# Cross-attention and an FP4 feed-forward layer: FFN rows handled last, the logits' scale moved, FFN weights quantised in five passes, loops written out

## The reference

```python
q = einsum('bnd,hdk->bhnk', layernorm(x), proj_q) + bias_q
k, v = the same of ctx with proj_k, bias_k and proj_v, bias_v
attn = softmax(einsum('bhqk,bhnk->bhqn', q, k) / sqrt(64))
x = x + (attn @ v, heads side by side) @ w_out.T
gate = fp4_linear(layernorm(x), w_gate); up = fp4_linear(layernorm(x), w_up)
x = x + fp4_linear(silu(gate) * up, w_down)
```

## Time and profile before

| | us |
|---|---|
| median of 3 runs | 460.31 (457.93 to 460.86) |
| the profiled execution | 461.22 |
| its span in the profile | 459.4 |
| granted TensorE clock, mean | 0.97 of full |
| busy: PE / DVE / ACT / POOL | 392.6 / 374.7 / 275.6 / 207.9 |

### The profile page before, as it was taken

One profiled execution on the slowest core, in us unless ns is written; L12 is line 12 of the kernel. 1 busy time (PEld: TensorE's weight loads), 2 busy tenths in 40 slices (PEclk: granted clock), 3 DMA queues, 4 the chain that ended last, 5 costly groups with the idle time before them and its releaser, 6 DMA issues.

```text
span 459.4 us, 10202 instructions
## 1 busy us (share of the span) xinstructions
PE 392.6 (85%) x3581; PEld 307.5 (67%) x3581; DVE 374.7 (82%) x752; ACT 275.6 (60%) x853; POOL 207.9 (45%) x177
## 2 busy tenths in 40 slices
PE   1889749999989999999899999997487897788956
PEld 1558637877868768778687788885255665566744
DVE  2799886797896997988969979777878898988791
ACT  3498756678766876777677776865323435424321
POOL 8240033254253352452542624413456778787841
PEclk9999987999999999999999999999888999999997
DMA  7950000000000000000000000000000000000011
GB/s 245 318 204 1 2 0 1 2 1 1 3 0 0 0 0 0 0 0 0 0 0 0 1 1 1 1 1 0 1 1 0 13 24 11 23 11 19 17 34 36
DMA packets 8406, 11.18 MB, mean 24 GB/s; under 512 B 499, under 2 KB 6335, under 8 KB 8383
## 3 DMA queue, kind: packets, MB, share of 16 engines
q1 hardware_dynamic: 8383, 10.88, 7.4%
HBM read 8.78 MB, written 2.10 MB: 24 GB/s over the span
## 4 chain that ended last, share of the span: by engine, by line
DVE 38%; PE 30%; issue 13%; POOL 10%; ACT 6%; DMA 1%; POOLq 1%; DVEq 0%; SPq 0%; ACTq 0%
PE ps L357 8%; PE ps L359 7%; PE ps L358 7%; DVE negmax L924 5%; DVE arena L936 4%; PE ps L457 3%; DVE arena L915 3%; POOL arena L1192 3%; PE ps L449 3%; DVE vw L869 2%; POOL arena L1234 2%; DVE arena L980 2%; ACT arena L677 2%; POOL arena L1238 1%; DVE arena L963 1%
## 5 line engine op out<-in xcount | busy, mean ns | idle before, releaser
L1184 POOL TENSOR_TENSOR arena<-arena,rinv 128x616 f32<-128x616 f32 x64 | 77.6, 1212 | 165.0 <-DVE rinv L932 165.0
L677 ACT ACTIVATE arena<-ps,ebias 128x154 f32<-128x154 f32 x256 | 96.4, 397 | 27.6 <-DVE ebias L927 27.3
L357 PE MATMUL ps<-vw,arena 128*128 128x256 f16 (+1 forms) x352 | 98.1, 279 | 15.5 <-DVE arena L936 6.4
L358 PE MATMUL ps<-vw,arena 128*128 128x256 f16 (+1 forms) x352 | 97.9, 278 | 0.0
L359 PE MATMUL ps<-vw,arena 128*128 128x256 f16 (+1 forms) x352 | 97.7, 278 | 0.0
L687 ACT ACTIVATE arena<-ps 128x512 f16<-128x512 f32 x80 | 48.5, 606 | 25.9 <-PE ps L457 25.3
L936 DVE TENSOR_TENSOR arena<-ps,arena 128x512 f16<-128x512 f32 x80 | 54.1, 676 | 8.5 <-ACT arena L687 7.9
L357 PE MATMUL ps<-arena,xnT_h 128*128 128x352 f16 x128 | 41.5, 324 | 16.4 <-DVE xnT_l L1023 14.6
L677 ACT ACTIVATION_READ_ACCUMULATOR arena<-ps,ebias 128x1 f32 x256 | 54.7, 214 | 0.0
L924 DVE TENSOR_REDUCE negmax<-ps 128x4 f32<-128x616 f32 x64 | 50.6, 791 | 4.3 <-PE ps L449 3.0
L457 PE MATMUL ps<-ident,arena 128*128 128x128 f32 x320 | 52.3, 287 | 0.0
(11 more groups left out here) (136 smaller groups left out, 935.8 us busy)
## 6 DMA issues: line engine op xcount, KB each, us to landing
out_dram<-arena SPq DMA_DIRECT2D x16, 128.0 KB, 1.7
xs<-in_x_dram SPq DMA_DIRECT2D x2, 896.0 KB, 10.2
arena<-in_L_xattn_w_out_dram SPq DMA_DIRECT2D x1, 1024.0 KB, 6.5
wffn<-in_L_ffn_w_down_dram SPq DMA_DIRECT2D x1, 704.0 KB, 7.6
wffn<-in_L_ffn_w_gate_dram SPq DMA_DIRECT2D x1, 640.0 KB, 10.8
wffn<-in_L_ffn_w_up_dram SPq DMA_DIRECT2D x1, 640.0 KB, 5.5
vw<-in_ctx_dram SPq DMA_DIRECT2D x1, 308.0 KB
xs<-in_x_dram SPq DMA_DIRECT2D x2, 128.0 KB, 5.0
```

What stands on the lines that cost most here:

```text
L357: pe.matmul(o, a_h, b_h, start=start, stop=False)
L358: pe.matmul(o, a_h, b_l, start=False, stop=False)
L677: last = act.activation(prob[:, s, h * L:(h + 1) * L], ps[:, 2 * (j % 2) + k % 2, (k // 2) * L:(k // 2 + 1) * L], ACT.Exp, bias=ebias[:, s ...
L1184: pool.tensor_tensor(v, v, rinv[:, s, 4 * j:4 * j + 4].unsqueeze(2).to_broadcast([P, 4, L]), ALU.mult).then_inc(normed, 1)
```

## The change

- **FFN's next rows last**: `magnitude_x(i+1)`, `grid_x(i+1)` and `round_x(i+1)` move from the head of the step's first half to behind `magnitude_h`, `grid_h` and `round_h` of the half before. The values are the same.
- **Logits' scale in the rows**: the normalised rows are split after multiplication by XS = 1/8; `proj_q` and `proj_k` are no longer multiplied by 16, their biases by 1/8 and 1. `ebias` (64 instructions of 128 x 4 on DVE) and `scale_proj("q")` go.
- **Weights in five passes**: `weights_value` and the four-pass rounding on DVE and POOL are replaced by what the rows of the FFN already use: `value` on POOL (s = 1, between the norms j = 1 and j = 2), |v| on ACT (g = 3), `minus_grid` on DVE (g = 4, behind `p_low`), and one multiplication on POOL.
- **Scale limit**: the second instruction of `block_scales` becomes a scalar_tensor_tensor that reads 1e-12 from a tile `least`.
- **Loops written out**: `steps` becomes a plain loop for all engines, and so do the stores.

```diff
-    for i in range(first):
-        body(i)
-    with eng.Fori(first, last) as i:
-        body(i)
-    for i in range(last, STEPS):
+    for i in range(STEPS):
         body(i)
...
@@ scalar
+                        if s == 1 and g == 3 and not (isinstance(i, int) and i >= W_STEPS):
+                            act.wait_ge(wvalued, i + 1)
+                            act.activation(wtmp[2], wtmp[0], ACT.Abs, scale=GRID).then_inc(wmagic, 1)
...
-                    if s == 0 and exists(i + 1): magnitude_x(i + 1)
                     silu_gate(i, s)
...
                     if exists(shift(i, s, -1)[0]): magnitude_h(*shift(i, s, -1))
+                    if s == 0 and exists(i + 1): magnitude_x(i + 1)
@@ vector
-                dve.wait_ge(max_done, n)
-                dve.tensor_scalar(ebias[:, s, 4 * j:4 * j + 4], negmax[:, s, 4 * j:4 * j + 4], LOGIT, None,
-                                  ALU.mult).then_inc(ebias_ready, 1)
...
-                dve.tensor_scalar(scale, amax, SIXTH, 1e-12, ALU.mult, ALU.max).then_inc(done, 1)
+                dve.scalar_tensor_tensor(scale, amax, SIXTH, least[:, 0:amax.shape[1]], ALU.mult, ALU.max).then_inc(done, 1)
...
-                        if w and g == 2: weights_value(i)
-                        if w and g == 3: weights_to_grid(i)
+                        if w and g == 4:
+                            dve.wait_ge(wmagic, i + 1)
+                            minus_grid(wtmp, wsummed, wgrid, i)
...
-                if p == 0: scale_proj("q", ld_q)
...
-                    if s == 0 and exists(i + 1): grid_x(i + 1)
                     hidden(i, s)
...
                     if exists(shift(i, s, -1)[0]): grid_h(*shift(i, s, -1))
+                    if s == 0 and exists(i + 1): grid_x(i + 1)
@@ gpsimd
+                        if s == 1 and j == 1 and not (isinstance(i, int) and i >= W_STEPS):
+                            value(wtmp[0], wffn[:, bass.ds(i * WSLICE, WSLICE)], [blk_w[:, r] for r in range(4)],
+                                  wscaled, wlowered, wvalued, i)
...
-                        pool.tensor_tensor(wtmp[1], wtmp[1], wtmp[2], ALU.subtract).then_inc(wq_round, 1)
...
-                    if s == 0 and exists(i + 1): round_x(i + 1)
                     if not last_tile(i, s): value_h(i, s)
                     if s == 1 and exists(i + 2): value_x(i + 2)
                     if exists(shift(i, s, -1)[0]): round_h(*shift(i, s, -1))
+                    if s == 0 and exists(i + 1): round_x(i + 1)
```

More of the change, by code:

```diff
@@ L133, in xattn_ffn_kernel @@
         below = sb("below", [P, 1], F32)
+        least = sb("least", [P, F // BLOCK], F32)
         unused = sb("unused", [P, 2], F32)
@@ L345, in store @@
                     sp.dma_start(out[s, bass.ds(i * P, P), :], y[:, s, :]).then_inc(stored[s], 16)
-            with sp.Fori(0, STEPS) as i:
+            for i in range(STEPS):
                 store(i)
@@ L648, in x_high @@
                 act.wait_ge(xt_mm, i + 1)
-                act.activation(xnT_h[:, :, :].rearrange("p c t -> p (c t)"), ps[:, Q_BANK, :], ACT.Copy).then_inc(xt_high, 1)
+                act.activation(xnT_h[:, :, :].rearrange("p c t -> p (c t)"), ps[:, Q_BANK, :], ACT.Copy,
+                               scale=XS).then_inc(xt_high, 1)
             x_high(0)
@@ L678, in exps @@
                                           ps[:, 2 * (j % 2) + k % 2, (k // 2) * L:(k // 2 + 1) * L],
-                                          ACT.Exp, bias=ebias[:, s, h:h + 1], scale=LOGIT,
+                                          ACT.Exp, bias=negmax[:, s, h:h + 1],
                                           accum_out=rsum[:, s, h:h + 1])
@@ L696, in weights_high @@
                         w = min(4, W1T - j0) * P
-                        last = act.activation(w1_h[:, c, j0 * P:j0 * P + w], o[:, 0:w], ACT.Copy, scale=FS)
+                        last = act.activation(w1_h[:, c, j0 * P:j0 * P + w], o[:, 0:w], ACT.Copy, scale=-FS)
                     else:
@@ L700, in weights_high @@
                             m = min(P, F - (j0 + k) * P)
-                            last = act.activation(wdT[0:m, j0 + k, 0:D], o[0:m, k * D:(k + 1) * D], ACT.Copy, scale=FS)
+                            last = act.activation(wdT[0:m, j0 + k, 0:D], o[0:m, k * D:(k + 1) * D], ACT.Copy, scale=-FS)
                     last.then_inc(wt_high, 1)
@@ L812, in _ @@
             dve.wait_ge(job_mm, J_BIAS + 1)
-            dve.tensor_scalar(biasT[:, :], bank(J_BIAS)[:, 0:3 * PAIRS], WS, None, ALU.mult).then_inc(bias_ready, 1)
+            for n, scale in enumerate((XS, 1.0, WS)):
+                last = dve.tensor_scalar(biasT[:, n * PAIRS:(n + 1) * PAIRS], bank(J_BIAS)[:, n * PAIRS:(n + 1) * PAIRS],
+                                         scale, None, ALU.mult)
+            last.then_inc(bias_ready, 1)
             dve.wait_ge(bias_ready, 1)
@@ L821, in _ @@
                 dve.wait_ge(w_high, c + 1)
-                last = dve.scalar_tensor_tensor(heads_of(wk_l, c), by_chunk("k")[:, c], WS, heads_of(wk_h, c),
+                last = dve.scalar_tensor_tensor(heads_of(wk_l, c), by_chunk("k")[:, c], 1.0, heads_of(wk_h, c),
                                                 ALU.mult, ALU.subtract)
@@ L993, in weights_low @@
                         w = min(4, W1T - j0) * P
-                        last = dve.scalar_tensor_tensor(w1_l[:, c, j0 * P:j0 * P + w], o[:, 0:w], FS,
+                        last = dve.scalar_tensor_tensor(w1_l[:, c, j0 * P:j0 * P + w], o[:, 0:w], -FS,
                                                         w1_h[:, c, j0 * P:j0 * P + w], ALU.mult, ALU.subtract)
@@ L1163, in _ @@
             pool.memset(below[:, :], BELOW)
+            pool.memset(least[:, :], 1e-12)
             pool.memset(ident[:, :], 0.0).then_inc(ident_zero, 1)
```

48 lines of the change are left out of this document (13 added, 35 removed).

## The result

The changed kernel takes 470.35 us (median of 4 runs, 468.68 to 471.32), the kernel before 460.38 (457.93 to 460.86): ratio 1.022 with the interval 1.019 to 1.026. The forecast was 468.7. The profiled execution of after took 469.99 us, its span is 467.9 against 459.4, so 8.5 us are to be found.

What follows compares the result with a forecast made beforehand. PE was taken as nearly the bound in attention, a chain through four engines in the FFN. From the profiled 461.2, -1.5 - 3.0 + 12.9 gives 469.6, less 0.9 to the median: 468.7 us; 8-in-10 range 452 to 474.

Steps and rivals of the forecast that it cites:

- The sign: Whole kernel: the change makes it slower; slower by over 1% was given 0.53.
- the mechanism in the FFN: FFN: grid_x takes turns with POOL, hidden(i,1) comes at 8.95 us, PE waits 3.2 us, its clock drops; +12.9 us.
- The two terms of attention: Setup and attention: logits' scale -1.5 us, weights in five passes -3.0 us (0.5 in each of six steps).
- The clock's term: FFN steps 2 to 6: half clock behind PE's 3.2 us wait loses 1.65 us a step on the chain.
- - 0.6: Start of the FFN: the first hidden comes 0.6 us earlier, without grid_x(1) ahead of it.
- Clock holds: FFN, rival: the clock stays full and steps 2 to 6 take 16.7 us; 460.2 us in total, chance 0.25.
- Relief carries through: FFN and attention, rival: grid_x slips in where POOL is idle, DVE's work bounds the FFN step; 449 us, chance 0.21.
- Late code: Whole program, rival: each of 16 written-out steps stops once for code, at 1 us; 484 us, chance 0.04.

Runs made afterwards that it cites:

- e2: The kernel before with only the three calls for the FFN's next rows moved last; median 471.26 us, four runs of 465.98 to 474.35, no ratio given.
- e4: The changed kernel, order untouched, plus 16 unread transposes of the identity on PE where it would wait for round_x; 460.06 us, ratio 1.004.
- e1_rows_first: The changed kernel with the three calls for the FFN's next rows back at the head of the step; 455.99 us, ratio 0.994.
- e11_logits_scale_alone: The kernel before with only the logits' scale taken into the rows and the loops written out; 449.97 us without one outlier, ratio 0.978.
- e3_only_written_out: The kernel before with only the loops over steps written out; 459.45 us over 8 runs, ratio 1.003.
- e8_ebias_again: The changed kernel with the FFN's rows first again and the ebias copy (times 1.0) back on DVE; 461.96 us, ratio 1.007.
- e7: The changed kernel with the FFN's rows first again and the weights quantised in six passes again; 451.94 us, ratio 0.984.
- e10_five_in_the_gap: The changed kernel with the FFN's rows first again and the weights' five passes moved one place earlier in the attention step; 449.40 us, ratio 0.977.
- e5_rows_in_the_middle: The changed kernel with the three calls for the FFN's next rows behind scales_h but ahead of the calls for h; 459.61 us, ratio 1.000.

## Why the prediction was right

The sign, the mechanism in the FFN and the total (468.7 against 470.35) held. The two terms of attention were right in their sum and wrong as prices of the two edits. That the total came so close is in part luck: the FFN's shortfall of 2.7 us was made up by a gain of 2.2 behind the last `hidden` that was not in the forecast.

- *FFN's rows last*, +13.5 between the `hidden`: measured +16.2. Its working holds nearly line by line. `grid_x` takes turns with POOL's two products (1.87, 1.75), `hidden(i,1)` comes at 8.76 (worked out: 8.95), PE waits 3.0 to 3.7 us (3.2), and the clock falls. With the clock held the step is 17.1 us (e2, e4) where 16.7 was worked out: over steps 2 to 6 that is 2.0 of the missing 2.7 us. The clock's term, 1.65 us a step, came from one stretch behind a wait of 2.36 us and was right on average, though not step by step: these five steps take 94.3 us in after and 85.5 in e4_fill_the_wait, 1.75 us each. In after the mean clock is 0.91 in one step and 0.82 in the next, so that they last 18.3 and 19.4 us by turns instead of 18.4.
- *Behind the last `hidden`* nothing was forecast, and 2.2 us were won. In before, a wait of 3.03 us there was followed by half clock, in after one of 3.17 us was not. In e1_rows_first a wait of 3.17 us at the same place was followed by half clock. So this gain is luck: nothing in the change is known to earn it.
- *Logits' scale*, -1.5: the step that failed is "in attention this is DVE time behind which PE seldom waits". In e11_logits_scale_alone the first `hidden` starts at 305.0, in e3_only_written_out at 313.0, so the scale is worth 8 us up to there, 7.3 of them in the six steps of the table (by the medians, 449.97 against 459.45, it is 9.5). The price taken was what the copy costs DVE, start to start (0.08 us). What it costs the chain is what ACT waits for it. The prediction had seen the copy of 1.62 us beside POOL's L1212, and ACT waits 2.28 us behind it, but counted its absence as part of what lets `add_attention` come earlier with five passes. One copy a step is held so in before (1.45 us beyond its 0.17), two in e8_ebias_again (1.5 us); a step without the copies is 1.2 to 1.3 us shorter. The holds alone would be enough for that, but no run has the copies without them, so how much is the hold and how much the second handover is not shown. In the view of the waits from 90 to 240 us, some five steps, ACT waited 16.4 us for it in before, 14 times; in e11_logits_scale_alone, 3.0 us for the maximum itself:

```profile
ACT arena L677 <- DVE ebias L927: 16.4, 14, 2.3
```
```profile
ACT arena L674 <- DVE negmax L924: 3.0, 5, 0.6
```

- *Weights in five passes*, -3.0 (bounds 0 and -9): measured +4.1 (e1 against e7) and +2.5 (e8 against e3) by the medians, 0.7 us a step in both, outside the bounds and of the other sign. The step that failed is what the gain was put down to. `add_attention` was to come 0.3 to 0.5 us earlier, and it does: it starts 14.94 us behind the block scales in e1_rows_first (163.03 - 148.09) against 15.48 in before (165.99 - 150.51). But with the copies gone and six passes kept it starts at 13.47 (e11), and with five passes and the copies at 16.12 (e8): the missing copies give 2 us, and the five passes take most of it back. The two passes were seen to stand ahead of the next row maximum and the hold by POOL's norm was right (1.13 us), but what waits for that maximum, ACT's exponentials for 1.98 us, was not followed, and a bound of 0 excluded a loss with no reason given.
- Together the terms gave -4.5 - 0.6 = -5.1 against -5.5 at the first `hidden`: the chain of a step had been worked out with both edits in it, and a step won 0.76 us, 0.21 of them by the loops, where 0.5 was forecast. From the result alone both terms would have passed as right; only runs with one edit undone showed them.
- *Scale limit* 0: right as far as it can be told (1.27 against 1.26; 451.94 against 449.97). *Loops* 0: right for the time (1.003), and the 0.21 us of an attention step is inside the bounds of 0.3. The Trainium skill (Runtime: NRT & Kernel Launch, "Instruction fetch mechanics") holds that taken branches risk a stall and that written-out code is fetched ahead. The 0.21 us that an attention step got shorter is in that direction; no view here ties it to fetching, the FFN's steps did not get shorter, and the kernel as a whole is neither faster nor slower by more than 0.6%.
- *Clock holds* (460.2): e4_fill_the_wait is that rival made real, at 460.06. *Relief carries through* (449) did not happen in the FFN; e10_five_in_the_gap comes to its number by attention instead. *Late code* (484): no step of e3_only_written_out is longer than before's by more than 0.01 us.

## What to carry to other kernels

Price an instruction between two engines by who waits for its result, not by its own length: a copy of usually 0.17 us, eight times a step and held by POOL once or twice, cost 1.2 to 1.3 us a step, and two passes fewer cost time because they stood ahead of what ACT waited for; look for the idle gap in the timeline and put them there. Where TensorE's wait grows to about 3 us in each round of a loop, count the clock as a cost of its own, and as a source of scatter. And undo edits one at a time even when the total fits the forecast: here an edit worth some 8 us hid that another cost 4 where it stood.

## What the runs showed of the hardware that was not expected

- The length of a single wait doesn't settle the clock. Followed by half clock: 2.36 us (before), 3.02 and 3.69 (after), 3.16 (e2_only_rows_last), 3.03 (end of before), 3.17 (end of e1_rows_first). Not followed by it: 3.09 and 3.10 (e2_only_rows_last), 3.17 (end of after). In e5_rows_in_the_middle no wait is above 1.4 us in a step whose mean clock is 0.90; there a wait of 1.36 us is followed 1.6 us later by one of 1.18, while in e4_fill_the_wait a single one of 1.35 us a step left the clock at 1.00. What decides between them no run here shows. The Trainium skill (TensorE: Matmul & The Clock Gate, "What's actually happening") says that the point at which the clock changes differs from run to run of the same kernel. The four runs of e2_only_rows_last fit that, with mean clocks of 0.945 to 0.974; where in them it changed is known of one alone.
- TensorE can be kept at 2.4 GHz by work that nobody reads: 16 transposes a step gave 10.3 us.
- DVE and POOL alternate when DVE queues instructions with two SBUF inputs and POOL instructions that read SBUF: two passes of 0.63 and 0.69 us became 1.87 and 1.75, each let through behind one of POOL's. A small `tensor_scalar` with its one tensor input in SBUF was held too: 0.17 us became 1.62 (before), 1.10 and 0.75 (e8_ebias_again), each until POOL's instruction ended.

Not tried: the move with five passes in the gap, and a filling of the waits that the FFN's first two steps have in every version.
